# Spectral filter: two groups of loads ahead of a store, and two GpSimd steps of the first MLP's last chunk moved

## The chip, the cores and the metric

The kernel runs on one core of a Trainium2 chip. The metric is the device time of one execution in microseconds (us). Before the change it is 1062.75 us, the median of three runs (1061.52 to 1064.59). A core has five engines that run side by side and wait for each other by semaphores: PE (matmul), DVE (VectorE), ACT (ScalarE), POOL (GpSimd) and SP, which here only issues DMAs, one after the other from one instruction stream.

## The reference

The input is one image of 48 x 48 tokens with 192 channels. It passes through two layers. Layer 0 is a transformer block: layer norm, attention of 12 heads with relative positions, projection, layer norm, MLP with GELU. Layer 1 is a spectral block (AFNO):

```
residual = x
h = layernorm(x, g1, be1)
xf = rfft2(h)                       # 48 x 25 frequencies x 192
o1 = relu(xf * w1 + b1)             # complex, 8 blocks of 24 channels
o2 = softshrink(o1 * w2 + b2, 0.01)
h = irfft2(o2) + h
h = h + residual
residual = h
m = layernorm(h, g2, be2)
return gelu(m @ fc1_w + fc1_b) @ fc2_w + fc2_b + residual
```

## The kernel before, in words

The work has four stages in a row. The first 780 us or so are the projections to q, k and v and the attention; the change touches nothing in them. Then come the three stages that matter here.

**The first MLP** (`block0` on each engine) goes through the 2304 tokens in NC = 6 chunks of 4 x 96 tokens. For a chunk c, PE makes the up product in HM = 6 tiles (`up`), ACT applies the GELU to each tile (L1089, `hid_f`) and rounds it to f16 (L1083, the first half of `hid`), and the f16 remainder "lo" = `hid_f` - `hid` is made by POOL for tiles 0 to 3 (`lo_of_hidden`, L898) and by DVE for tiles 4 and 5 (L1683). All six count on the semaphore `mlp0_lo`. PE's down product (`down`) first takes the rounded halves of tiles t = 0 and 2, and then waits for all six lo parts of the chunk before it goes on (the wait on `lo` in L1432). Its end lets DVE form `y_sb` (L1675), take its statistics (L94 to L102), and write the normed `h1` in two steps (L1697, L1705). Between them POOL computes the inverse root (L120). The semaphore `h1_ok` says that `h1` is there. POOL then adds `r3` = `h1` + `y_sb` (`skip`, L920), and DVE may not write the next chunk's `y_sb` before that is done (`r3_ok`). PE transforms `h1` of a chunk along the width (`dft`, L1442), ACT copies it out (`spectrum`, L1100) and SP stores it to DRAM (`u1_d`).

The last chunk has no next chunk to prepare, so that its order is shorter. POOL does lo of four tiles, `skip` of chunk 4, the root of chunk 5, then two small memsets (L927), the copy of the second filter bias over the group's frequencies (`f_b2`, L928), `skip` of chunk 5 and a memset (L931), which gives `f_pads`. PE does `down` of chunk 5, `dft(4)`, 34 products whose results nobody reads (`stay_awake`, which keep PE busy), `dft(5)` and 44 more of them.

**The spectral filter** goes through 25 frequencies in G = 5 groups g. For each group SP loads 2 x 48 rows of the width spectrum (`f_load`, L743, into `f_in`, which has two buffers), PE transforms along the height (`transform`, L1486, 80 matmuls), ACT copies it (L1117), PE multiplies by w1 (`layer1`), ACT applies the relu (L1134), PE multiplies by w2 (`layer2`, L1509, 80 matmuls), DVE adds the bias and shrinks (L1716, L1720, L1723), PE transforms back (`inverse`, 4 matmuls), ACT copies into `f_u` (L1123, one buffer), and SP stores that in `u2_d` (`f_store`, L750). PE's order in the loop is: layer1(g), transform(g+1), inverse(g-1), layer2(g). At the end stand 14 unread products, inverse(4) and 42 unread products.

SP's order here is a short loop. After the loads of groups 0 and 1 it does, for each g, the load of g+2 (once transform(g) has freed its buffer, semaphore `fh_ps`), and then the store of g (once ACT has filled `f_u`, semaphore `fu_ok`).

**The second MLP** (`block1`) is the same kind of loop as the first, after a transform back along the width.

Of the kernel before, what the change touches and what calls it, by code (L numbers as in the profile page):

```python
# [41 lines left out]
NC = NT // CT  # L42
CW = CT * T
HID = 4 * C
HM = HID // 128
# [21 lines left out]
G = KF // KG  # L67
# [10 lines left out]
def chunks(body):  # L78

    for c in range(NC):  # L80
        body(c, c + 1 < NC)
# [35 lines left out]
def norm_root(pool, nc, rstd, sem, n):  # L117

    pool.wait_ge(sem["var"], n + 1)
    nc.gpsimd.tensor_tensor(rstd[:, 1, :], rstd[:, 0, :], rstd[:, 2, :], ALU.pow).then_inc(sem["rstd"], 1)  # L120


def build(nc, d, out):
    ctx = ExitStack()
    with ctx:
# [3 lines left out]
        def sem(name):  # L129
            return ctx.enter_context(nc.semaphore(name))  # L130
# [185 lines left out]
        up0 = {k: sem(f"mlp0_{k}") for k in ("up_ps", "act", "hi", "lo", "dn_ps", "sum")}  # L316
# [113 lines left out]
        def is_at(n, head):  # L430

            return isinstance(n, int) and n == head
# [68 lines left out]
        def _(sp):  # L501
# [239 lines left out]
            def f_load(g):  # L741
                for r in range(2):
                    sp.dma_start(f_in[r * S:(r + 1) * S, g % 2, 0:KG * C],  # L743
                                 u1_d[:, r, ds(g * KG, KG), :].rearrange("h f c -> h (f c)"))\
                      .then_inc(f_in_ok[g % 2], 16)

            def f_store(g):
                sp.wait_ge(fu_ok, g + 1)
                for r in range(2):
                    sp.dma_start(u2_d[:, r, ds(g * KG, KG), :],  # L750
                                 f_u[r * S:(r + 1) * S, :, :]).then_inc(fu_out, 16)
# [3 lines left out]
            for g in range(G):  # L755
                if g + 2 < G:
                    sp.wait_ge(fh_ps, g + 1)
                    f_load(g + 2)
                f_store(g)
            sp.wait_ge(fu_out, 32 * G)  # L760

            def load_u2(c):
# [32 lines left out]
        def _(pool):  # L795
# [99 lines left out]
            def lo_of_hidden(c, sems, tiles=range(HM)):  # L895
                for m in tiles:
                    pool.wait_ge(sems["hi"], c * HM + m + 1)
                    nc.gpsimd.tensor_tensor(hid[:, m, 1, :], hid_f[:, m, :], hid[:, m, 0, :],  # L898
                                            ALU.subtract).then_inc(sems["lo"], 1)

            def bias_into(c, row, norm, done):

                pool.wait_ge(norm["out"], c + 1)
                x1_c = x1[:, ds(c * CT, CT), :]
                nc.gpsimd.tensor_tensor(x1_c, x1_c, rows[0:T, row:row + 1, :].to_broadcast([T, CT, C]),
                                        ALU.add).then_inc(done, 1)

            def block0(c, more):
                lo_of_hidden(c, up0, range(POOL_TILES))
                if more:  # L910
                    norm_root(pool, nc, rstd, ln2, c + 1)
                    bias_into(c + 1, 0, ln2, x1b_ok)
                if not is_at(c, 0):
                    skip(c - 1)
                norm_root(pool, nc, rstd, ln3, c)

            def skip(c):

                pool.wait_ge(h1_ok, c + 1)
                nc.gpsimd.tensor_tensor(r3[:, ds(c * CT, CT), :], h1[:, :, :], y_sb[:, :, :],  # L920
                                        ALU.add).then_inc(r3_ok, 1)

            norm_root(pool, nc, rstd, ln2, 0)
            bias_into(0, 0, ln2, x1b_ok)
            chunks(block0)
            for b in range(2):
                nc.gpsimd.memset(f_in[:, b, KG * C:KG * C + FPAD], 0.0)  # L927
            nc.gpsimd.tensor_copy(f_b2[:, :, :, :], f_b2s[:, :].rearrange("p (g c) -> p g c", g=FG).unsqueeze(2)  # L928
                                  .to_broadcast([FP, FG, KG, FC])).then_inc(f_b2_ok, 1)
            skip(NC - 1)  # L930
            nc.gpsimd.memset(f_a[:, 2 * FN:2 * FN + FPAD], 0.0).then_inc(f_pads, 1)  # L931

            def bias_into_wide(c):
# [911 lines left out]
```

## Time and profile before

| | |
|---|---|
| median of 3 runs | 1062.75 us (1061.52 to 1064.59) |
| profiled execution | 1060.05 us, span of the trace 1058.2 us |
| mean granted clock of PE | 0.967 of full speed |
| busy share | PE 95%, DVE 81%, ACT 66%, POOL 32% |
| first MLP and what is before it, until DVE ends h1 of chunk 5 | to 898.7 us |
| spectral filter, first load's issue to last store's landing | 904.9 to 963.2 us |

The times inside are microseconds from the span's start, of one profiled execution. A busy PE isn't PE at its peak, and the unread products count as busy as well. So the share of busy time tells little in the two stages of interest, and the rows with an idle time at their end (in square brackets, with what ended it) tell more. The rows print tile names without buffer numbers and digits (`u_d` is `u1_d` or `u2_d`, `f_b` is `f_b1` or `f_b2`, `r` is `r3`, `h` is `h1`). L1156 is the line of a helper for all plain matmuls, which the tile names tell apart.

### The profile page before, as it was taken

The numbers are of one execution on the slowest core, as the hardware profiler recorded it, in microseconds if no ns is written. First come the engines' busy times: TensorE is split into PE (matmuls) and PEld (weight loads), VectorE is DVE, ScalarE is ACT, GpSimd is POOL, SyncE is SP. The second block draws the span as 40 slices with busy tenths as digits, with TensorE's granted clock in tenths as the row PEclk, the third lists the DMA queues.
The fourth block names the chain that finished last, engine by engine and source line by source line (L and its number), as shares of the span: only waits on it lengthen the run. The fifth ranks groups of instructions, "written<-read, shape, count | busy, mean of one in ns | idle before, by whom it ended". The sixth has DMA issues, their size and how long they took to land.

```text
span 1058.2 us, 36799 instructions
## 1 busy us (share of the span) xinstructions
PE 1004.9 (95%) x15948; PEld 708.1 (67%) x15948; DVE 853.0 (81%) x1741; ACT 701.0 (66%) x1004; POOL 337.7 (32%) x161
## 2 busy tenths in 40 slices
PE   5988999999999999999999999999988998978998
PEld 3556267777776767677777777676647776754666
DVE  4859999999999999999999999999626767132664
ACT  3767077777787777777777778787774543231555
POOL 4440242232444342424343332324224554000111
PEclk9985599999999999999999999999999999999999
DMA  4787764443423231313131413122100100222231
GB/s 118 199 209 224 208 165 128 130 109 73 104 65 84 67 86 57 90 51 96 46 101 43 99 45 96 51 62 62 51 13 12 47 23 25 59 68 75 80 91 57
DMA packets 75158, 91.80 MB, mean 87 GB/s; under 512 B 15341, under 2 KB 67378, under 8 KB 74805
## 3 DMA queue, kind: packets, MB, share of 16 engines
q1 hardware_dynamic: 74967, 89.45, 31.2%
q8 instruction: 125, 2.05, 0.8%
q14 instruction: 36, 0.29, 0.1%
q10 hardware_dynamic: 30, 0.02, 0.0%
HBM read 65.63 MB, written 23.21 MB: 84 GB/s over the span
## 4 chain that ended last, share of the span: by engine, by line
PE 78%; DVE 10%; DMA 4%; ACT 4%; issue 2%; POOL 1%; SPq 1%; DVEq 0%; ACTq 0%
PE ps L1161 41%; PE ps L1321 19%; PE ps L1156 14%; DVE stage_lo L1597 2%; DVE mx_p L1628 2%; ACT hid_f L1089 1%; DVE stats L94 1%; PE ps L1174 1%; POOL rstd L120 1%; DVE xh L112 1%; PE ps L1267 1%; PE ps L1486 1%; DMA f_in<-u_d 1%; DMA u_sb<-u_d 1%; ACT hid L1083 1%
## 5 line engine op out<-in xcount | busy, mean ns | idle before, releaser
L1628 DVE TENSOR_REDUCE mx_p<-ps 128x1 f32<-128x464 f32 (+1 forms) x1080 | 607.0, 628 | 15.7 <-PE ps L1161 5.3
L1036 ACT ACTIVATE prob<-ps 128x768 f32<-128x768 f32 x648 | 495.4, 810 | 164.6 <-PE ps L1161 164.3
L1161 PE MATMUL ps<-kc,qc 112*32 112x464 f16 (+1 forms) x4320 | 457.1, 369 | 3.0 <-DVE stage_lo L1597 2.9
L1161 PE MATMUL ps<-qv,ka 113*32 113x384 f16 x5184 | 400.3, 327 | 2.6 <-ACT prob L1036 2.3
L835 POOL COPY qv<-qv 48x6144 f16<-48x6144 f16 x36 | 190.8, 5301 | 349.4 <-DMA qv<-kq_d 349.1
L1321 PE MATMUL ps<-prob,v_ext 128*32 128x384 f32 x2592 | 289.4, 485 | 0.5 <-ACT prob L1036 0.5
L1161 PEld LDWEIGHTS ps<-qv,ka 113*32 113x32 f16 x5184 | 214.5, 97 | 75.6 <-issue 17.9
L1161 PEld LDWEIGHTS ps<-kc,qc 112*32 112x32 f16 x4320 | 172.8, 95 | 100.1 <-DVE mx_p L1628 27.1
L1321 PEld LDWEIGHTS ps<-prob,v_ext 128*32 128x32 f32 x2592 | 117.2, 110 | 11.9 <-ACT prob L1036 1.2
L1156 PE MATMUL ps<-xnt_all,w_up 96*128 96x384 f16 x432 | 75.0, 326 | 2.8 <-ACT hid_f L1089 2.8
L120 POOL TENSOR_TENSOR rstd<-rstd 96x4 f32<-96x4 f32 x24 | 27.0, 1124 | 158.6 <-DVE rstd L102 158.0
L1156 PE MATMUL ps<-w_dn,hid 128*96 128x192 f16 (+1 forms) x756 | 66.4, 246 | 5.2 <-DVE hid L1683 2.9
L1156 PEld LDWEIGHTS ps<-w_dn,hid 128*96 128x96 f16 (+1 forms) x756 | 62.4, 112 | 10.0 <-issue 6.1
L1089 ACT ACTIVATE hid_f<-ps,b_up 128x384 f32<-128x384 f32 x72 | 40.5, 580 | 41.1 <-PE ps L1156 41.0
L1156 PEld LDWEIGHTS ps<-xnt_all,w_up 96*128 96x128 f16 x432 | 41.4, 98 | 34.2 <-ACT hid_f L1089 5.5
L1606 DVE TENSOR_TENSOR xnt_all<-xnt_f,xnt_all 96x768 f16<-96x768 f32 x12 | 13.2, 1100 | 40.3 <-ACT xnt_all L1028 40.3
L1024 ACT ACTIVATE xnt_f<-ps,shift,gain 96x384 f32<-96x384 f32 x24 | 14.7, 662 | 40.7 <-PE ps L1174 40.7
L1716 DVE TENSOR_TENSOR f_y<-ps,f_b 112x960 f32<-112x960 f32 x5 | 5.8, 1158 | 43.2 <-PE ps L1509 43.2
L849 POOL COPY v_ext<-v_all 128x288 f32<-128x288 f32 x12 | 5.0, 425 | 99.3 <-PE ps L1321 99.2
L1083 ACT ACTIVATE hid<-hid_f 128x384 f16<-128x384 f32 x72 | 35.9, 516 | 0.0
L1683 DVE TENSOR_TENSOR hid<-hid_f,hid 128x384 f16<-128x384 f32 x48 | 26.8, 588 | 10.7 <-ACT hid L1083 10.7
L1597 DVE TENSOR_TENSOR stage_lo<-ps,stage_hi 96x864 f16<-96x864 f32 x32 | 31.0, 1045 | 3.5 <-ACT stage_hi L1005 3.5
(107 smaller groups left out, 827.6 us busy)
## 6 DMA issues: line engine op xcount, KB each, us to landing
qv<-rel_d SPq DMA_DIRECT2D x216, 144.0 KB
qc<-rel_d SPq DMA_DIRECT2D x22, 216.0 KB, 4.0
xin<-in_x SPq DMA_DIRECT2D x12, 288.0 KB, 3.5
kq_d<-khl SPq DMA_DIRECT2D x24, 144.0 KB, 2.2
q_h<-kq_d SPq DMA_DIRECT2D x9, 288.0 KB, 4.6
q_w<-qw_d SPq DMA_DIRECT2D x9, 288.0 KB, 6.5
rel_d<-stage_hi SPq DMA_DIRECT2D x4, 648.0 KB, 7.3
rel_d<-stage_lo SPq DMA_DIRECT2D x4, 648.0 KB, 8.9
```

Source lines behind the costliest of these rows:

```text
L120: nc.gpsimd.tensor_tensor(rstd[:, 1, :], rstd[:, 0, :], rstd[:, 2, :], ALU.pow).then_inc(sem["rstd"], 1)
L835: nc.gpsimd.tensor_copy(qv[0:3 * HD, b, 1:NV, :], qv[0:3 * HD, b, 0:1, :].to_broadcast([3 * HD, NV - 1, QW])).then_inc(q_wide, 1)
L1024: nc.scalar.activation(xnt_f[:, k, :], ps[0:C2, bank + k, 0:CW], ACT.Identity, bias=shift[1 + i][:, k:k + 1], scale=gain[1 + i][:, k:k + 1])\
L1036: nc.scalar.activation(prob[:, s4(p, s), :].rearrange("p (a b) -> p a b", a=2), ps[:, 3 + 2 * (s % 2):5 + 2 * (s % 2), 0:CW], ACT.Exp).the ...
L1083: nc.scalar.activation(hid[:, m, 0, :], hid_f[:, m, :], ACT.Copy).then_inc(sems["hi"], 1)
L1089: nc.scalar.activation(hid_f[:, m, :], ps[:, m % 2, 0:CW], ACT.Gelu, bias=b_up[i][:, m:m + 1], scale=1 / WS).then_inc(sems["act"], 1)
L1156: return nc.tensor.matmul(o, l, r, start=start, stop=stop)
L1161: ins = nc.tensor.matmul(ps[c:c + 32, bank, 0:w], l[:, c:c + 32], r, start=True, stop=True, tile_position=(0, c))
L1321: ins = nc.tensor.matmul(ps[r:r + 32, 7, 0:CW], v_ext[:, p, (s + e) % GS, :], prob[:, s4(p, s + e), j * CW:(j + 1) * CW], start=(s % GS == ...
L1597: nc.vector.tensor_tensor(out_lo, x, out_hi, ALU.subtract).then_inc(op_lo, 1)
L1628: nc.vector.tensor_reduce(mx_p[:, q * GT + k // MP, k % MP:k % MP + 1], ps[:, slot, 0:min(MW, N - k % MP * MW)], AX, ALU.max).then_inc(uni ...
L1683: nc.vector.tensor_tensor(hid[:, m, 1, :], hid_f[:, m, :], hid[:, m, 0, :], ALU.subtract).then_inc(sems["lo"], 1)
```

## The change

It has two parts.

In SP's loop of the spectral filter, the store of group g-1 instead of g stands behind the load of g+2, and the last store stands behind the loop. Each load keeps its wait for a free buffer. On SP, from the load of group 2 on, before (the words in brackets are the semaphores that are waited for; a group has two DMAs, one for each part of the spectrum):

```order
L743 DMA f_in<-u1_d 48x960 [waits fh_ps]
L743 DMA f_in<-u1_d 48x960
L750 DMA u2_d<-f_u 48x960 [waits fu_ok]
L750 DMA u2_d<-f_u 48x960
L743 DMA f_in<-u1_d 48x960 [waits fh_ps]
L743 DMA f_in<-u1_d 48x960
L750 DMA u2_d<-f_u 48x960 [waits fu_ok]
L750 DMA u2_d<-f_u 48x960
L743 DMA f_in<-u1_d 48x960 [waits fh_ps]
L743 DMA f_in<-u1_d 48x960
```

and the same place of SP now:

```order
L743 DMA f_in<-u1_d 48x960 [waits fh_ps]
L743 DMA f_in<-u1_d 48x960
L743 DMA f_in<-u1_d 48x960 [waits fh_ps]
L743 DMA f_in<-u1_d 48x960
L750 DMA u2_d<-f_u 48x960 [waits fu_ok]
L750 DMA u2_d<-f_u 48x960
L743 DMA f_in<-u1_d 48x960 [waits fh_ps]
L743 DMA f_in<-u1_d 48x960
L750 DMA u2_d<-f_u 48x960 [waits fu_ok]
L750 DMA u2_d<-f_u 48x960
```

The load of group 3 now stands ahead of the store of group 0, and the load of group 4 ahead of the store of group 1.

In POOL's stream at the last chunk of the first MLP, `skip` of chunk 4 now waits for all six lo parts of chunk 5 too, and `skip` of chunk 5 stands ahead of the two memsets and the copy of the bias. On POOL, before:

```order
L898 TENSOR_TENSOR hid<-hid_f,hid 128x384 [waits mlp0_hi] x4
L920 TENSOR_TENSOR r3<-h1,y_sb 96x768 [waits h1_ok]
L120 TENSOR_TENSOR rstd<-rstd 96x4 [waits ln3_var]
L927 MEMSET f_in 96x16 x2
L928 COPY f_b2<-f_b2s 112x960
L920 TENSOR_TENSOR r3<-h1,y_sb 96x768 [waits h1_ok]
L931 MEMSET f_a 112x16
```

and now (the line numbers have moved by two to five):

```order
L900 TENSOR_TENSOR hid<-hid_f,hid 128x384 [waits mlp0_hi] x4
L924 TENSOR_TENSOR r3<-h1,y_sb 96x768 [waits h1_ok,mlp0_lo]
L120 TENSOR_TENSOR rstd<-rstd 96x4 [waits ln3_var]
L924 TENSOR_TENSOR r3<-h1,y_sb 96x768 [waits h1_ok]
L932 MEMSET f_in 96x16 x2
L933 COPY f_b2<-f_b2s 112x960
L935 MEMSET f_a 112x16
```

The first sum has one more wait, and the second sum has come in front of the memsets and the copy. The instructions of PE, DVE and ACT and their order are the same in both kernels.

The diff:

```diff
@@ SP, spectral filter
                 if g + 2 < G:
                     sp.wait_ge(fh_ps, g + 1)
                     f_load(g + 2)
-                f_store(g)
+                if g > 0:
+                    f_store(g - 1)
+            f_store(G - 1)
             sp.wait_ge(fu_out, 32 * G)
@@ POOL, first MLP
                 if not is_at(c, 0):
+                    if not more:
+                        pool.wait_ge(up0["lo"], NC * HM)
                     skip(c - 1)
                 norm_root(pool, nc, rstd, ln3, c)
...
             chunks(block0)
+            skip(NC - 1)
             for b in range(2):
                 nc.gpsimd.memset(f_in[:, b, KG * C:KG * C + FPAD], 0.0)
             nc.gpsimd.tensor_copy(f_b2[:, :, :, :], ...).then_inc(f_b2_ok, 1)
-            skip(NC - 1)
             nc.gpsimd.memset(f_a[:, 2 * FN:2 * FN + FPAD], 0.0).then_inc(f_pads, 1)
```

## Rows read from the trace of the kernel before

**Rows 1.** The page: busy time (sum, share, count); granted clock in 40 slices.

```profile
PE 1004.9 (95%) x15948; PEld 708.1 (67%) x15948; DVE 853.0 (81%) x1741; ACT 701.0 (66%) x1004; POOL 337.7 (32%) x161
...
PEclk9985599999999999999999999999999999999999
```

**Rows 2.** Chain of waits, 875 to 968 us: start, us, what.

```profile
884.77 2.58 DVE hid L1683 x2
887.39 5.47 PE ps L1156 x52
...
893.75 7.00 PE ps L1156 x38
...
926.21 3.08 DMA f_in<-u_d
```

**Rows 3.** DVE by time, 862 to 970: start, us, instruction [idle <-releaser].

```profile
884.70 2.64 DVE L1683 TENSOR_TENSOR hid<-hid_f,hid 128x384 f16<-128x384 f32 x2
891.59 0.95 DVE L1675 SCALAR_TENSOR_TENSOR y_sb<-ps,x 96x768 f32<-96x768 f32 x1 [4.25 <-PE ps L1156]
...
894.37 2.86 DVE L1697 SCALAR_TENSOR_TENSOR xh<-y_sb,mv,rows 96x192 f32<-96x192 f32 x4
897.27 1.40 DVE L1705 SCALAR_TENSOR_TENSOR h<-xh,rstd,rows 96x192 f32<-96x192 f32 x4
```

**Rows 4.** All engines by time, 885.5 to 888: DVE's second lo tile.

```profile
885.17 2.17 DVE L1683 TENSOR_TENSOR hid<-hid_f,hid 128x384 f16<-128x384 f32 x1
```

**Rows 5.** DVE's L1683 in all of the first MLP: ns min/median/max, first and last start.

```profile
L1683 DVE TENSOR_TENSOR hid<-hid_f,hid x12: 542/552/2172, 796.1 to 885.2; 128x384 f16<-128x384 f32 x12
```

**Rows 6.** POOL by time, 862 to 970.

```profile
884.85 2.07 POOL L920 TENSOR_TENSOR r<-h,y_sb 96x768 f32<-96x768 f32 x1 [0.62 <-DVE h L1705]
...
895.71 0.98 POOL L928 COPY f_b<-f_b2s 112x960 f32<-112x960 f32 x1
898.75 1.80 POOL L920 TENSOR_TENSOR r<-h,y_sb 96x768 f32<-96x768 f32 x1 [2.06 <-DVE h L1705]
```

**Rows 7.** PE by time, 862 to 970.

```profile
887.39 4.16 PE L1156 MATMUL ps<-w_dn,hid 128*96 128x192 f16 x48 [1.88 <-DVE hid L1683]
...
899.29 1.46 PE L1156 MATMUL ps<-h,dft_w 96*100 96x384 f32 x4
...
913.87 2.00 PE L1486 MATMUL ps<-dft_h,f_in 96*48 96x48 f32 x80
...
921.88 1.85 PE L1156 MATMUL ps<-f_o,dft_hi 112*96 112x480 f32 x4
...
925.59 1.88 PE L1156 MATMUL ps<-f_x,f_w 112*112 112x240 f32 x8
929.33 2.00 PE L1486 MATMUL ps<-dft_h,f_in 96*48 96x48 f32 x80 [1.86 <-DMA f_in<-u_d]
...
939.70 2.15 PE L1486 MATMUL ps<-dft_h,f_in 96*48 96x48 f32 x80 [2.85 <-DMA f_in<-u_d]
941.79 3.33 PE L1156 MATMUL ps<-f_o,dft_hi 112*96 112x480 f32 x4
...
950.20 1.85 PE L1156 MATMUL ps<-f_o,dft_hi 112*96 112x480 f32 x4 [1.34 <-DVE f_o L1723]
```

**Rows 8.** SP's DMA issues by time, 862 to 970.

```profile
904.85 7.21 SPq L743 DMA_DIRECT2D f_in<-u_d  x6
924.82 0.77 SPq L750 DMA_DIRECT2D u_d<-f_u  x2
925.63 1.01 SPq L743 DMA_DIRECT2D f_in<-u_d  x2
...
935.02 2.04 SPq L743 DMA_DIRECT2D f_in<-u_d  x2
```

**Rows 9.** Stretches: us, busy PE, PEld, DVE, ACT, POOL, granted clock, DMA share, GB/s.

```profile
941.80:945.10 3.30, 3.30 (x8) 1.00 (x8) 0.00 (x0) 0.97 (x1) 0.00 (x0) 0.54 0.02 5
945.10:950.20 5.10, 3.76 (x89) 3.16 (x88) 2.98 (x3) 2.33 (x6) 0.00 (x0) 1.00 0.27 72
```

## The prediction

> **What bounds the kernel now.** I read the page first, for the share of each engine and the granted clock by slice [rows 1]. PE is busy for 95% of the span and its clock is at or near full speed from the sixth slice on, so the attention, three quarters of the span, is PE's own work, and the change doesn't touch it. What an edit of the last 180 us is worth has to be read there, step by step. So I went to the chain of waits between 875 and 968 us [rows 2]: it runs through DVE's two lo tiles of the last chunk, then PE's down product with the first transform behind it, PE's unread products, and in the filter through a load of `f_in`. Then I took each engine's own order of time in that stretch. DVE [rows 3] and POOL [rows 6] show that the second lo tile lies beside POOL's sum. PE [rows 7] shows three idle times that the edits could reach: 1.88 us until DVE's lo tile, 1.86 us until the load of group 3, and 2.85 us until the load of group 4. SP [rows 8] shows why these loads are late: each is issued right behind a store.
>
> **Part one, the lo tile.** DVE starts its two lo tiles at 884.70 [rows 3]. The second alone starts at 885.17 and takes 2.17 us, to 887.34 [rows 4]. The same instruction has a median of 0.552 us over the twelve of this stage and a minimum of 0.542; only this one is at 2.172 [rows 5]. POOL's sum of chunk 4 starts at 884.85 and ends at 886.92 [rows 6], inside the slow one. PE starts again at 887.39, 0.05 us behind the tile [rows 7].
>
> Now the sum waits for all six lo parts. The second tile then takes 0.55 us, ends at 885.72, and PE starts at 885.77 instead of 887.39. The term is 2.17 - 0.55 = **1.62 us**. From both sides: it can't be more than PE's whole idle time there, 1.88, and is 0 if the tile is slow for a reason of its own. I take 1.62, since one in twelve is slow and it is the one with the sum beside it.
>
> The Trainium skill ("SBUF — State Buffer", section "Who interferes with whom") says that a DVE instruction with both inputs in SBUF and a GpSimd instruction that reads SBUF don't share: the one that issues second is blocked until the first has ended. By it the tile would begin its work only at 886.92 and end 0.5 us later; the trace has 0.42 us, so it agrees. It also says what the moved sum costs: nothing, if DVE stands still while it runs, and its whole length if not.
>
> That is the point to look at next, for the added wait holds POOL. Behind the sum are queued the root of chunk 5 and the second sum, and DVE's `y_sb` of chunk 5 waits for the first sum. The sum now runs from 885.8 to about 887.6 or 887.9 (1.80 to 2.07 us [rows 6]). DVE is idle from its lo tile until PE ends the down product: before 4.25 us, until 891.59 [rows 3], now until 891.59 - 1.62 = 889.97. So the sum is done 2.1 us or more before anyone asks for it, and beside idle DVE. The root is asked for about 2.7 us later still. The wait costs nothing.
>
> **Part two, the sum and the copy of the bias.** In the norm of chunk 5, DVE's four L1697 take 2.86 us [rows 3] against 1.40 for the four L1705 of the same size; POOL's root and its copy of the bias, 0.98 us at 895.71 [rows 6], lie beside them. Without the copy `h1` ends up to 1 us earlier. But PE isn't waiting for it: `h1` ends at 898.67 [rows 3], and PE starts the transform of chunk 5 at 899.29 [rows 7], directly behind its 34 unread products, which are fixed in number and lie on the chain [rows 2]. The 0.6 us that DVE is ahead becomes about 1.5, and the term is **0**. The cover of the 34 products is what makes it nothing; without them the gain would be up to 1 us. On the other side, the copy and the memset that gives `f_pads` come later: second sum 1.80 us after `h1`, then 0.98 and some 0.3 for the memsets. With `h1` between 896.1 and 897.1 (898.67 less 1.62 and up to 1) that is done by 900.2 at the latest, while PE needs `f_pads` for the first filter product only at 908.47 less 1.62 us. That costs nothing. The 1.62 us of part one does pass through, because everything behind the lo tile is a chain of PE, ACT and DMA without a fixed time in it.
>
> **Part three, the loads.** Before, the load of group 3 is issued at 925.63 behind the store of group 0 at 924.82 [rows 8] and lands 3.08 us after its second issue, at 929.29 [rows 2]. Its buffer was free when transform(1) ended, at 913.87 + 2.00 = 915.87 [rows 7]; the loads of groups 0 to 2 were all issued by 912.06 [rows 8]. Now it is issued at 915.9, with about 4 us to land lands by 920, and PE wants it behind layer1(2), which starts at 925.59 and takes 1.88, at 927.47. The wait of **1.86 us** goes, with 7 us to spare. The load of group 4 was issued at 935.02 behind the store of group 1. Now only the store of group 0 is ahead of it, so that it goes out where the load of group 3 did, at 925.63, and lands at 929.3. PE wants it at 927.47 + 2.00 + 1.85 + 2.00 + 1.88 = 935.2 less the overlaps, some 935.0. The wait of **2.85 us** goes too, with over 5 us to spare. The stores: that of group 1 was 934.21 and its `f_u` is now ready about 1.9 us earlier; each is issued once its `f_u` is full, since the load ahead of it waits only for a transform that PE did before. So no store is later than its data. What is late next is PE itself: with no wait a round of the filter is 2.00 + 1.85 + 2.00 + 1.88 us of products, while DVE needs 2.98 us in a round [rows 9] and ACT copies and relus beside it. The wait of 1.34 us for DVE's shrink in the last round [rows 7] stays.
>
> **Part four, the clock.** Behind the idle time of 2.85 us the granted clock was 0.54 from 941.80 to 945.10, near the level of 1.2 GHz, and back at 1.00, 2.4 GHz, after it [rows 9]. There transform(4) took 2.15 against 2.00 us and inverse(2) 3.33 against 1.85 [rows 7]. With neither idle time in front of it PE has products to do without a break from transform(1) at 913.87 to the last round, so I expect full clock: 0.15 + 1.48 = **1.63 us**. From both sides: 0 if the clock falls elsewhere in the stage for as long, or didn't fall in the timed runs; about twice that if those runs had it worse.
>
> The Trainium skill ("TensorE: Matmul & The Clock Gate", section "What's actually happening") says that the activity watch runs free of the kernel, so that the moment of a change differs from execution to execution. By it this term belongs to one execution and need not be in the median. No row here tells, since the profile is of one execution.
>
> **The sum.** 1.62 + 1.86 + 2.85 + 1.63 = 7.96 us. From the profiled execution's 1060.05 us (span 1058.2 and 1.85 around it) that gives 1052.1. The median is 2.70 above the profiled execution, and I add that back: 1062.75 - 7.96 = 1054.8, said as 1055.
>
> **Rivals.**
> The clock term isn't there: all as above without part four, a gain of 6.3 us, 1056.4. For it: the fall is seen once; against it: the two idle times ahead of it are the longest of PE in these rounds [rows 7], and both go.
> The lo tile stays slow, or PE finds another wait in its place. The gain is 7.96 - 1.62 = 6.3 us, 1056.4. Against it stand eleven fast tiles of twelve.
> The loads land no earlier than PE's next wait: if the chain from layer2 over DVE's shrink to inverse, which costs 1.34 us in the last round, took over in rounds 2 and 3, one would get back 4.7 - 2 x 1.34 = 2.0 us of part three and nothing of part four. With part one some 3.1 us at most are left (2.0 to 3.6): 1059.7, no change that can be told. Against it: inverse(0) at 921.88, in a round whose load was in time, had no such wait [rows 7], because transform and layer1 stand between layer2 and inverse.
> Slower: PE's clock falls in the filter and stays low for most of it, because the moved idle times meet it at another place. The price by the rows is 1.48 us more for each 1.85 us of products. To end 3.2 us above the time before it has to eat 6.3 + 3.2 = 9.5 us, so it decides from about 12 us of products at half clock on, a round and a half; at two rounds, 15 us of products, it costs 12 and the time is 1062.75 - 6.3 + 12 = 1068. Against it: PE has fewer idle times than before at every place, and with more of them its clock was low for 3.3 us only [rows 9].
>
> **Chances, range.** Forecast 0.62; no clock term 0.20; lo tile 0.08; the loads mostly hidden 0.07; slower 0.03. The first three are faster: 0.90, within 0.3% (3.2 us, about what can be told from no change) 0.07, slower 0.03. The range starts from the extremes of the runs: the largest gain, 1.88 + 4.71 + 1.63 = 8.2, from the profiled 1060.05 gives 1051.9; the smallest of the first three cases, 6.3, from the highest run gives 1058.3. I say 1051.8 to 1058.6.
>
> **What would show it.** Right: no idle time with `f_in` as its releaser in front of the transforms of groups 3 and 4; loads of group 3 issued about 3 us behind those of group 2; granted clock 1.00 through the filter; L1683 at 0.55 us in the last chunk, and PE's down product going on about 1.6 us sooner; PE's first transform of the filter 1.6 us earlier, and the last inverse 8 us earlier. Wrong: a new idle time of PE before an inverse in rounds 2 and 3, a slow L1683 with POOL idle, DVE waiting for `r3` in front of `y_sb`, or a second MLP longer than before.

## The result, and the profile after

| | before | changed |
|---|---|---|
| median of 4 runs | 1062.7 us (1061.52 to 1064.59) | 1050.09 us (1048.78 to 1051.88) |
| profiled execution | 1060.05 us | 1051.88 us |
| span of the trace | 1058.2 us | 1050.1 us |

The ratio is 0.9885, with a 95% interval of 0.9851 to 0.9919: 12.6 us between the medians, 9 to 16 by the interval. The forecast was 8.0 us, 1055 in the range from 1051.8 to 1058.6. So the direction was right, and the median lies 1.7 us below the range. Between the two profiled executions the difference is 8.2 us, nearly what the sum had. That these two differences, 12.6 and 8.2 us, lie so far apart is the question of this text.

In the trace, all four places that the prediction went through look as it said, but that DVE gains 1.46 us in the norm instead of "up to 1". The first group is PE's order of time in the changed kernel, 862 to 970 us, which answers to [rows 7] (L1160 is the helper of all plain matmuls now, L1490 the forward transform of the filter):

```profile
885.96 4.16 PE L1160 MATMUL ps<-w_dn,hid 128*96 128x192 f16 x48 [0.25 <-DVE hid L1687]
...
897.85 1.46 PE L1160 MATMUL ps<-h,dft_w 96*100 96x384 f32 x4
...
906.97 2.54 PE L1490 MATMUL ps<-dft_h,f_in 96*64 96x48 f32 x80 [0.52 <-DMA f_in<-u_d]
...
924.10 1.87 PE L1160 MATMUL ps<-f_x,f_w 112*112 112x240 f32 x8
925.90 2.00 PE L1490 MATMUL ps<-dft_h,f_in 96*48 96x48 f32 x80
...
933.36 2.00 PE L1490 MATMUL ps<-dft_h,f_in 96*48 96x48 f32 x80
935.29 1.85 PE L1160 MATMUL ps<-f_o,dft_hi 112*96 112x480 f32 x4
...
942.23 1.85 PE L1160 MATMUL ps<-f_o,dft_hi 112*96 112x480 f32 x4 [1.34 <-DVE f_o L1727]
```

PE waits 0.25 us instead of 1.88 ahead of the rest of the down product. The transforms of groups 3 and 4, at 925.90 and 933.36, have no idle time ahead of them, take 2.00 us, and inverse(2) takes 1.85 instead of 3.33. The wait of 1.34 us for DVE's shrink stays.

DVE and POOL, the same stretch, for [rows 3] and [rows 6]:

```profile
884.89 1.01 DVE L1687 TENSOR_TENSOR hid<-hid_f,hid 128x384 f16<-128x384 f32 x2
890.15 0.95 DVE L1679 SCALAR_TENSOR_TENSOR y_sb<-ps,x 96x768 f32<-96x768 f32 x1 [4.25 <-PE ps L1160]
...
892.94 1.40 DVE L1701 SCALAR_TENSOR_TENSOR xh<-y_sb,mv,rows 96x192 f32<-96x192 f32 x4
894.37 1.40 DVE L1709 SCALAR_TENSOR_TENSOR h<-xh,rstd,rows 96x192 f32<-96x192 f32 x4
```

```profile
885.98 1.81 POOL L924 TENSOR_TENSOR r<-h,y_sb 96x768 f32<-96x768 f32 x1 [1.56 <-DVE hid L1687]
...
895.86 1.82 POOL L924 TENSOR_TENSOR r<-h,y_sb 96x768 f32<-96x768 f32 x1 [1.63 <-DVE h L1709]
...
897.71 0.98 POOL L933 COPY f_b<-f_b2s 112x960 f32<-112x960 f32 x1
```

The two lo tiles take 1.01 us together instead of 2.64, and the sum has moved behind them, to 885.98, where DVE stands still until 890.15. The four L1701 take 1.40 us instead of 2.86, so that `h1` ends at 895.77 (894.37 + 1.40), 2.1 us ahead of PE's transform at 897.85 (before 0.6).

SP's issues, for [rows 8]:

```profile
903.43 11.76 SPq L743 DMA_DIRECT2D f_in<-u_d  x8
923.32 0.77 SPq L750 DMA_DIRECT2D u_d<-f_u  x2
924.13 1.00 SPq L743 DMA_DIRECT2D f_in<-u_d  x2
```

Four groups of loads have been issued before the first store, where it was three, and the fifth goes out at 924.13, 9.2 us ahead of its transform at 933.36.

### The profile page after: what moved, and what is told of

It reads as the page before. It is cut to its first block, busy times and chain, and to the rows that moved or that the text cites. A ratio compares the mean times of both kernels' runs of the same rounds, so it can differ in the third digit from the quotient of the medians.

```text
span 1050.1 us, 36800 instructions
## 1 busy us (share of the span) xinstructions
PE 1002.8 (95%) x15948; PEld 707.7 (67%) x15948; DVE 849.3 (81%) x1741; ACT 700.5 (67%) x1004; POOL 337.4 (32%) x161
## 3 DMA queue, kind: packets, MB, share of 16 engines
q8 instruction: 125, 2.05, 0.8%
## 4 chain that ended last, share of the span: by engine, by line
PE 78%; DVE 11%; DMA 4%; ACT 4%; issue 2%; POOL 1%; SPq 0%; DVEq 0%; ACTq 0%
PE ps L1165 40%; PE ps L1325 19%; PE ps L1160 14%; DVE mx_p L1632 2%; DVE stage_lo L1601 2%; PE ps L1178 1%; ACT hid_f L1093 1%; DVE stats L94 1%; POOL rstd L120 1%; DVE xh L112 1%; PE ps L1271 1%; PE ps L1490 1%; PE ps L1513 1%; ACT hid L1087 1%; DMA u_sb<-u_d 1%
## 5 line engine op out<-in xcount | busy, mean ns | idle before, releaser
L1165 PEld LDWEIGHTS ps<-kc,qc 112*32 112x32 f16 x4320 | 172.7, 95 | 100.2 <-DVE mx_p L1632 28.2
L1160 PE MATMUL ps<-xnt_all,w_up 96*128 96x384 f16 x432 | 75.0, 326 | 2.8 <-ACT hid_f L1093 2.8
L1160 PE MATMUL ps<-w_dn,hid 128*96 128x192 f16 (+1 forms) x756 | 67.7, 249 | 3.6 <-ACT hid L1087 2.2
L1160 PEld LDWEIGHTS ps<-w_dn,hid 128*96 128x96 f16 (+1 forms) x756 | 63.7, 114 | 8.3 <-issue 6.1
L1160 PEld LDWEIGHTS ps<-xnt_all,w_up 96*128 96x128 f16 x432 | 41.4, 98 | 34.2 <-ACT hid_f L1093 5.5
```

What stands on the lines that cost most here:

```text
L1160: return nc.tensor.matmul(o, l, r, start=start, stop=stop)
L1165: ins = nc.tensor.matmul(ps[c:c + 32, bank, 0:w], l[:, c:c + 32], r, start=True, stop=True, tile_position=(0, c))
```

## The experiments

**The same kernel, the change again, and two parts alone.** The four ran on one chip, against 24 runs of the kernel before. The first is the kernel before with no edit.

> The kernel before once more, against itself, on the same chip as the next three. Theory A (the four terms, 8.0 us in all, are what the change is worth, and the rest of the 12.6 us between the medians is what executions of one kernel differ by, in the stages ahead of the change): the medians of this and of the kernel before agree within 1.5 us, but single executions spread over 3 us or more. Theory B (the change is worth 12 us, because executions outside the profile lose more in the filter): the spread stays under 1 us at a given chip.

Measured: 1062.57 us against 1061.92, ratio 1.0001 (0.9979 to 1.0022), single executions from 1056.2 to 1066.2. So one kernel's executions differ by up to 10 us, and one profile is one draw out of that. Theory A has the spread right (over 3 us, with medians within 1.5), B had it wrong (under 1 us). But the trace of this execution, with the span of 1062.9 us, shows where much of the spread is, in PE's order of time in the filter:

```profile
922.44 1.87 PE L1156 MATMUL ps<-f_x,f_w 112*112 112x240 f32 x8
926.27 3.34 PE L1486 MATMUL ps<-dft_h,f_in 96*48 96x48 f32 x80 [1.95 <-DMA f_in<-u_d]
929.54 3.52 PE L1156 MATMUL ps<-f_o,dft_hi 112*96 112x480 f32 x4
932.98 2.12 PE L1509 MATMUL ps<-f_w,f_a 112*48 112x48 f32 x80
935.03 1.87 PE L1156 MATMUL ps<-f_x,f_w 112*112 112x240 f32 x8
939.87 3.29 PE L1486 MATMUL ps<-dft_h,f_in 96*48 96x48 f32 x80 [2.96 <-DMA f_in<-u_d]
943.09 3.52 PE L1156 MATMUL ps<-f_o,dft_hi 112*96 112x480 f32 x4
946.53 2.17 PE L1509 MATMUL ps<-f_w,f_a 112*48 112x48 f32 x80
```

The same trace by stretches (the columns of [rows 9]):

```profile
926.20:933.00 6.80, 6.73 (x86) 4.16 (x86) 0.00 (x0) 0.97 (x1) 0.00 (x0) 0.52 0.01 2
933.00:939.80 6.80, 3.91 (x89) 3.31 (x88) 2.98 (x3) 2.54 (x6) 0.00 (x0) 0.98 0.42 111
939.80:946.50 6.70, 6.63 (x84) 4.09 (x84) 0.00 (x0) 0.97 (x1) 0.00 (x0) 0.52 0.01 2
```

Behind both idle times the granted clock is 0.52, near the level of 1.2 GHz, and the products behind them take 3.3 and 3.5 us instead of 2.00 and 1.85. In the first profile this had happened behind one of the two only, and late: transform(4) took 2.15 us, and only inverse(2) behind it took 3.33 [rows 7], [rows 9].

The changed kernel again:

> The changed kernel again, with five rounds. Theory A: 6.5 to 9.5 us below the kernel before, near the 8.0 of the sum. Theory B: 11 to 13.5 us below it.

Measured: 1052.01 us (1049.77 to 1054.46), ratio 0.9912 (0.9885 to 0.9938), which is 9.3 us, 6.6 to 12. The medians themselves lie 9.9 us apart. That is at the upper end of A's band and below B's, but the interval reaches into both, and it overlaps that of the first comparison (9 to 16). This run doesn't decide between them.

The loads alone, which is the first hunk of the diff:

```diff
-                f_store(g)
+                if g > 0:
+                    f_store(g - 1)
+            f_store(G - 1)
```

> The kernel before with the stores in SP's loop one group later and nothing else. Theory A: 1.86 + 2.85 + 1.63 = 6.3 us below the kernel before; in the trace no idle time of PE ahead of the transforms of groups 3 and 4, and full clock through the filter. If the clock term isn't there: 4.7. Theory B puts the surplus of 4 us here: 10 to 11.

Measured: 1054.09 us, ratio 0.9935 (0.9912 to 0.9959), 6.9 us, 4.4 to 9.3. B's 10 to 11 us lie outside the interval, A's 6.3 inside. No idle time stands ahead of the two transforms, and the inverses of the loop take 1.85 us each, at a full clock.

The added wait of POOL alone:

```diff
+                    if not more:
+                        pool.wait_ge(up0["lo"], NC * HM)
```

> The kernel before with GpSimd's sum of chunk 4 waiting for the six lo parts of the last chunk, and nothing else. Theory A: 1.6 us below the kernel before, DVE's second lo tile at 0.55 us and PE's idle time at 0.25. Theory B, if the surplus is here: 5 to 6 us. Rival: the tile stays slow, no difference.

Measured: 1060.85 us, ratio 0.9993 (0.9973 to 1.0012), a difference of 0.7 us that may be anything from 2.9 us faster to 1.3 slower. The time rules out B's 5 to 6 us, but can't tell A's 1.6 us from nothing. The trace can: both lo tiles take 1.01 us, and PE goes on after 0.25 us instead of 1.88.

```profile
885.40 1.01 DVE L1685 TENSOR_TENSOR hid<-hid_f,hid 128x384 f16<-128x384 f32 x2
```

**The clock apart from the waits.** In the change, the idle times ahead of the transforms of groups 3 and 4 and the clock behind them go away together. To part them, the kernel before got unread products in the idle time, with the loads as late as ever:

```diff
                 layer1(g)
+                if g in (2, 3):
+                    pe.wait_ge(fy_ok, g)
+                    stay_awake((9, 15)[g - 2], 4, hid[:, 0, 0, :])
                 if g + 1 < G:
                     transform(g + 1)
```

> The kernel before with 9 and 15 unread products (0.16 us each, so 1.5 and 2.45 us) on PE in the idle time ahead of the transforms of groups 3 and 4; the loads stay as late as before, and what is computed is the same. Theory C, formed from the trace of the kernel before run again (the clock term isn't 1.63 us but what the two idle times happen to cost in an execution: 1.6 us in the first profile, 6.3 in the second, which is why the medians lie further apart than the profiles): the clock stays full, from the start of transform(0) to the start of inverse(4) it takes 42.2 + 4.7 = 46.9 us in the trace, and the median is 2 to 5 us below the kernel before. Theory A (clock term 1.6 us and the rest is variation ahead of the filter): 1 to 2 us below. Rival: the clock falls anyway, because unread products don't count, 0.

Measured: 1056.21 us against 1061.67, ratio 0.9953 (0.9936 to 0.997), 5.0 us, 3.2 to 6.8. This kernel does more work than the one before and waits for the same loads, and is faster all the same. PE's order of time in it:

```profile
923.70 1.63 PE L1156 MATMUL ps<-hid 128*128 128x384 f16 x9
925.75 2.00 PE L1486 MATMUL ps<-dft_h,f_in 96*48 96x48 f32 x80 [0.42 <-DMA f_in<-u_d]
...
933.11 2.60 PE L1156 MATMUL ps<-hid 128*128 128x384 f16 x15
935.88 2.00 PE L1486 MATMUL ps<-dft_h,f_in 96*48 96x48 f32 x80 [0.16 <-DMA f_in<-u_d]
```

From the start of transform(0) to that of inverse(4) it takes 46.82 us, with 46.9 expected. The granted clock is 1.00 over that stretch. Over the six executions of this kernel the mean granted clock was 0.971 or 0.972 in five and 0.966 in one; over the 17 of the kernel before on the same chip it was 0.971 or more in two.

So A's 1 to 2 us lie outside the interval, and C's 2 to 5 us inside: the waits for the loads are as long as ever, and with PE kept busy in them the clock doesn't fall behind them. That the idle times cost more by the clock than the 1.63 us of the first profile is shown. The size is less sure. The 5.0 us hold whatever else parts these executions (in this trace the stretch behind inverse(4) takes 100.6 us, in those of the kernel before 101.1 to 104.1), and the run with the loads alone, 6.9 us (4.4 to 9.3), has room for 4.6 of idle time and 3.5 of clock, but not quite for 4.6 and 5.0.

**The copy alone.** The diff is the move of `skip(NC - 1)` ahead of the memsets.

> The kernel before with only GpSimd's second sum moved ahead of the memsets and the bias copy. All theories: DVE's four L1697 shrink from 2.9 us to about 1.9 in the trace and h1 of the last chunk ends some 1 to 1.4 us sooner, while PE starts its transform behind the 34 unread products as before: 0 us (within 1). In the filter of this trace, the same as in the kernel before, theory C expects falls of the clock costing anything between 1.6 and 6.5 us.

Measured: 1061.56 against 1061.67 us, ratio 1.0002 (0.9987 to 1.0017), so no difference, within 1.4 us on one side and 1.8 on the other. The four L1697 take 1.40 us, where 1.9 was expected, and PE starts the transform directly behind its 34 products, as before. The term is 0, as predicted. In the filter of this trace the clock didn't fall at all, with idle times of 1.99 and 2.25 us: the surplus there is 0.15 us, where theory C expected 1.6 to 6.5. So in this point C's expectation failed: the cost can be nothing as well, and the later expectations of C start at 0.

**The cover taken away.** The changed kernel with fewer unread products, with the copy in its new and in its old place:

```diff
-            stay_awake(34, 4, hid[:, 0, 0, :])
+            stay_awake(22, 4, hid[:, 0, 0, :])
```

> The changed kernel with 22 instead of 34 unread products ahead of the transform of chunk 5. If these products are what hides DVE's gain (h1 ends 2.1 us ahead of PE in the trace of the changed kernel): 12 x 0.163 = 2.0 us below the changed kernel, so about 11.4 below the kernel before by the comparison just run. If PE's clock falls for want of them: no gain, or slower, with a granted clock under 1 behind the store of the last chunk.

> As the last one, but with the bias copy and memsets back ahead of the second sum, so that they lie beside DVE's norm again. If the copy is worth what DVE's time says once the cover is gone: PE waits about 1.2 us for h1 ahead of the transform of chunk 5, and this is 1.2 us slower than the run with 22 products before it. Rival: no wait, no difference.

Measured: 1048.34 us, ratio 0.9878 (0.9859 to 0.9897), which is 13 us below the kernel before (11 to 15, with 11.4 expected), and 1050.98 us, ratio 0.9898 (0.9881 to 0.9914). PE's order of time, the first and the second kernel:

```profile
891.46 3.75 PE L1160 MATMUL ps<-hid 128*128 128x384 f16 x22 [0.90 <-ACT u_sb L1104]
895.04 1.46 PE L1160 MATMUL ps<-h,dft_w 96*100 96x384 f32 x4
```

```profile
892.49 3.75 PE L1160 MATMUL ps<-hid 128*128 128x384 f16 x22 [0.90 <-ACT u_sb L1104]
897.46 1.53 PE L1160 MATMUL ps<-h,dft_w 96*100 96x384 f32 x4 [1.22 <-DVE h L1709]
```

The products went from 5.70 to 3.75 us, 1.95 less with 2.0 expected, and the granted clock behind them, from 895 to 902.8 us, is 1.00. With the copy in its old place PE waits 1.22 us for `h1`, the 1.2 that was expected; in its new place, not at all. So the copy's move is worth 1.2 us as soon as the products stop hiding it. The medians differ by 2.6 us, where 1.2 was expected, and their intervals overlap; the size is from the trace.

**One more idle time, and three more traces.** The changed kernel with 22 products, and 13 instead of 8 ahead of the second MLP:

```diff
-            stay_awake(8, 3, hid[:, 0, 0, :])
+            stay_awake(13, 3, hid[:, 0, 0, :])
```

> The changed kernel with 22 instead of 34 unread products, as before, and 13 instead of 8 unread products ahead of the second MLP, where PE waits for the second load of u_sb (0.5 to 2.5 us in the traces so far) and the clock fell in three of them. Theory C (idle time of PE costs by the clock what the execution's moment makes of it): the slow executions go, so the median is 0 to 1.5 us below the run with 22 products (1048.3, 12.9 below the kernel before) with a smaller spread. Rival: the five products delay the load's user and cost up to 0.8 us.

Measured: 1049.5 us (1045.96 to 1052.04), ratio 0.9876 (0.9848 to 0.9903). It can't be told from the run with 22 products, and its spread is wider, 6.1 us against 2.4, not smaller as expected. In its trace the idle time ahead of the second load's user is gone, but that this helps the time is not shown. Both versions have medians below the changed kernel's; the ratio of the run with 22 products, 0.9878, is lower than the changed kernel's two, 0.9885 and 0.9912 on other chips, but all these intervals overlap.

> The kernel before, one more trace. Theory C: from the start of transform(0) to the start of inverse(4) it takes 42.2 us and the two idle times (4.2 to 4.9) and between 0 and 7 us for the clock, another value in each trace. Theory A: 48.7 as in the first trace.

> The same once more: theory C another value between 46.4 and 54, theory A 48.7.

> The changed kernel, one more trace. Both: 42.2 us from the start of transform(0) to the start of inverse(4), as in the two traces so far, since no idle time over 1.4 us is left there.

Measured in one profiled execution each: 1062.85, 1061.99 and 1050.06 us. What they are for is this table, in us, each row from one trace where it names no more: the stretch from the start of transform(0) to the start of inverse(4), the two idle times ahead of transforms 3 and 4, what is left over 42.19 us and these idle times, and the stretch from the start of inverse(4) to the end of the span.

| trace | filter | idle | rest: clock | to the end |
|---|---|---|---|---|
| before, first profile | 48.67 | 1.86 + 2.85 | 1.77 | 101.1 |
| before, run again | 53.46 | 1.95 + 2.96 | 6.36 | 104.1 |
| wait of POOL only | 49.79 | 1.99 + 2.39 | 3.22 | 103.7 |
| copy only | 46.58 | 1.99 + 2.25 | 0.15 | 101.7 |
| before, third trace | 51.43 | 2.17 + 2.35 | 4.72 | 103.5 |
| before, fourth trace | 51.62 | 2.02 + 2.73 | 4.68 | 101.4 |
| changed, three traces | 42.19, 42.19, 42.18 | none | 0 | 100.9, 101.8, 101.2 |
| loads only | 42.19 | none | 0 | 106.7 |
| changed, 22 products: as it is, old place of the copy, 13 for 8 | 42.19, 42.18, 42.19 | none | 0 | 100.2, 100.5, 100.3 |

With the loads late, the filter takes 46.6 to 53.5 us, another value in each execution; with them early, it takes 42.18 or 42.19 in all seven. The third and fourth trace came out as theory C expected, and not at A's 48.7.

The table also says where the gain of the whole change lies. In the mean of the four traces of the kernel before and the three of the changed one, the span is 10.6 us shorter: 9.1 of it in the filter (4.7 of idle time and 4.4 of clock), 1.2 behind it, and 0.3 ahead of it, where the 1.6 us of the lo tile are hidden by starts of the filter that differ by 3 us between traces of one kernel (905.3 to 908.5, and 904.9 to 907.5).

## Why the prediction was wrong, by its own steps

**Part one, the lo tile: right.** 1.62 us was predicted, and PE's idle time went from 1.88 to 0.25, which is 1.63. The rival in which the tile stays slow is out: with the sum moved, and nothing else, the pair takes 1.01 us. The added wait of POOL cost nothing, as said: in the changed kernel the sum ran from 885.98 to 887.79, 2.4 us before DVE's `y_sb` at 890.15, which waits for it.

**Part two, the copy: right.** It is 0 behind 34 unread products and 1.2 us behind 22. Only what DVE gains was put too low: "up to 1 us", and it is 1.46.

**Part three, the loads: right.** 1.86 + 2.85 = 4.71 us; over the six traces with late loads the two idle times are 4.6 in the mean. The rival in which DVE's shrink takes over is out, since nothing waits for it in rounds 2 and 3. (Its price was summed wrongly: 1.62 + 2.0 leaves a gain of 3.6 us, 1059.1, not 3.1 and 1059.7. Nothing hangs on it.) The load of group 3 goes out 3.8 us behind the end of group 2's issues, at 914.42, where "about 3 us" stood.

**Part four, the clock: the step that failed.** It had 0.15 + 1.48 = 1.63 us and, as its bound, "about twice that if those runs had it worse". In the six traces the term is 1.77, 6.36, 3.22, 0.15, 4.72 and 4.68, 3.5 in the mean, and 5.0 (3.2 to 6.8) by the runs with the idle time filled. The sum with these is 1.6 + 4.6 + 3.5 = 9.7 us, or 11.2 with the 5.0. The two comparisons of the changed kernel gave 12.6 and 9.3 us, with intervals of 9 to 16 and 6.6 to 12, each of which holds both sums. So the mechanism was right, idle time of PE first and the clock behind it, and the term that was mis-sized is that of the clock. What is left of the 12.6 us, 1.4 to 2.9, is within the spread of executions and has no cause shown.

The upper bound could have been had from the rows at hand. There were two idle times, not one, and behind each stand 2.00 + 1.85 us of products; at the row's price of 1.48 for 1.85 us that is an estimate of 3.1 us each and 6.2 for both. The trace of the kernel before, run again, has 6.36. The prediction took the one fall in its one trace for the size of the term, gave it a rival for "not there" and none for "at both places". The range also left out its own bound: it took the largest gain as 8.2 us, with 1.63 for the clock. With twice that, 3.26, the largest gain is 9.85 and the range goes down to 1050.2, next to the measured 1050.09; with 6.2 it is 12.8, and the range goes down to 1047.3 and has the measured time inside.

The rule of the Trainium skill that was weighed there ("TensorE: Matmul & The Clock Gate", section "What's actually happening") has the moment of a change differ from execution to execution. The table agrees: in four executions of one program the term is 1.77, 6.36, 4.72 and 4.68. Why it differs no run here shows. The prediction drew only half of it: it had a rival and a chance for a term that is less than in the profile, and for one that is more it had the words "about twice that", which didn't reach its range.

**The base.** The sum was made against the profiled execution of 1060.05 us and hit that of the changed kernel by 0.2 us (1052.1 against 1051.88). That it came so near is luck in part: the start of the filter moved from 908.47 to 906.97 and the filter from 48.67 to 42.19 us, nearly the 1.62 and 6.34 of the sum, but other traces of the two kernels would have given differences from 6.8 to 14.6 us. Executions of the kernel before spread over 1056 to 1068 us in all these runs. The first profile had a cheap filter (1.77 us of clock) and a start of the filter at 908.47, which in the other traces of the kernel before came between 905.3 and 907.2. The 2.70 us that were added back for the median belong to this spread, and are no fixed offset of a kernel: in the changed kernel the profiled execution lies 1.79 us above the median. These two (2.65, with the median of four runs, and 1.79, about 4.4 together) are what parts 12.6 from 8.2. A part of them is the clock in the filter, which was cheap in the first profile (1.77 against 3.5 to 5).

**Still open.** What the stretch behind inverse(4) adds: it takes 100.2 to 104.1 us in most traces, and 106.7 in the one with the loads alone, where the clock was 0.60 from 968 to 972 and 0.65 from 972 to 982 us behind a wait for `u_sb`:

```profile
968.00:972.00 4.00, 3.17 (x6) 1.41 (x7) 0.81 (x2) 0.00 (x0) 0.00 (x0) 0.60 0.01 2
972.00:982.00 10.00, 9.86 (x43) 4.72 (x41) 5.76 (x18) 5.12 (x11) 1.01 (x1) 0.65 0.31 90
```

Both kernels have that wait. The clock fell behind it in four traces, those with a wait of 2.05 to 2.46 us (the loads alone, the wait of POOL only, the kernel before run again and its third trace), and in none of the ten with 1.95 or less, among them all three of the changed kernel. Whether it costs the changed kernel less often, which would add to its gain, three traces don't tell. In the filter the length alone doesn't decide: 1.95 us was followed by a fall, and 2.25 was not.

## What to carry to other kernels

An idle time of PE is priced twice: by its length, and by what the products behind it cost at the lower clock. The second price differs between executions, so a fair estimate of its upper end is that the clock falls behind every such idle time at once, worked out from the products behind each, even if the trace shows it at one of them only. When a change takes away such idle times, the gain in the median can exceed what one profile shows, and the test is to fill the idle time with unread products and leave the waits alone.

## What the runs showed of the hardware

Six traces with late loads have twelve idle times of 1.9 to 3.0 us in an otherwise busy PE. Behind eight of them, in five of the traces, the granted clock fell to about half (0.51 to 0.54 where it was low throughout a stretch) for all or a part of the products. Behind four (1.86, 1.99, 1.99 and 2.25 us) the products took their usual times, though three of these are longer than the shortest that was followed by a fall, 1.95. With 1.5 and 2.45 us of these idle times filled by unread products, the products behind them ran at full speed, and the kernel was 5 us faster for 24 more matmuls. One program's executions spread over 10 us on one chip, 1056.2 to 1066.2 (12 executions).

DVE's second lo tile ended 0.42 us after POOL's sum in the first trace, and takes 0.55 us without it. The norm shows something like it: its four instructions, of 0.35 us each, took 2.86 us with the memsets and the copy (0.98) behind the root, and 1.39 or 1.40 without them: eight traces have the old order and six the new one. That is 1.46 us more, beyond the copy's own length. Two of the four were slow, in the kernel before:

```profile
894.70 1.13 DVE L1697 SCALAR_TENSOR_TENSOR xh<-y_sb,mv,rows 96x192 f32<-96x192 f32 x1
...
895.76 1.14 DVE L1697 SCALAR_TENSOR_TENSOR xh<-y_sb,mv,rows 96x192 f32<-96x192 f32 x1
```

with POOL beside them:

```profile
894.54 1.12 POOL L120 TENSOR_TENSOR rstd<-rstd 96x4 f32<-96x4 f32 x1 [7.62 <-DVE rstd L102]
895.62 0.16 POOL L927 MEMSET f_in<- 96x16 f32 x2
895.71 0.98 POOL L928 COPY f_b<-f_b2s 112x960 f32<-112x960 f32 x1
```

The second of these two starts with the copy (895.71) and ends 0.2 us after it. The first ends at 895.83, when the root and the memsets end (895.66 and 895.78). In the changed kernel the root lies beside the same four instructions and costs them nothing:

```profile
893.11 1.12 POOL L120 TENSOR_TENSOR rstd<-rstd 96x4 f32<-96x4 f32 x1 [5.32 <-DVE rstd L102]
```

So it is the memsets and the copy together that cost the 1.46 us. They were always moved together, and what each costs, and how the first instruction comes to be slow before the copy begins, no run shows.
